# Four attention layers on one core: the last self-attention takes its output through plain values and a second projection, and two small parts of the earlier layers move

## The reference, cut to what matters

```python
x = L0(x, ctx)   # cross-attention with a causal mask, residual, LayerNorm; then gelu feed-forward
x = L1(x, ctx)   # cross-attention: scores * weights, mask; Wo, residual, LayerNorm
x = L2(x, ctx)   # cross-attention with a key mask; w_out, LayerNorm; relu feed-forward, LayerNorm
x = L3(x, ctx)   # self-attention, then a gated feed-forward
# L3, attention part (heads of 64 channels, segments of 64 tokens):
pooled = rms_norm(ctx.mean(axis=1)) ; k_c, v_c = split(pooled @ to_mem_tokens_w @ to_qkv_w)
xn = rms_norm(x, attn_norm_w)
q, k, v = split(xn @ to_qkv_w) ; q, k = rope(q), rope(k)
kf, vf = concat([k_c, persist, k]), concat([v_c, persist, v])
probs = softmax(mask(q @ kf.T * 64 ** -0.5))   # own segment, causal, plus memory and persistent keys
x = x + (probs @ vf).reshape(b, n, 1024) @ to_out_w
```

## Time and profile before

| | before |
|---|---|
| median of 3 runs | 2474.96 us (2472.53 to 2475.68) |
| the profiled execution | 2471.87 us, span 2470.1 us |
| instructions | 83369 |
| busy: TensorE matmul / weight load | 2308.8 us (93%) / 1812.7 us (73%) |
| busy: VectorE / ScalarE / GpSimd | 1888.0 (76%) / 1498.6 (61%) / 1559.2 us (63%) |
| mean granted TensorE clock | 0.985 |
| DMA moved | 211.78 MB, mean 86 GB/s |

### The profile page before, as it was taken

The page is one execution under the profiler, slowest core; times in us unless marked ns, Lnnn a source line. Parts: engine busy times, 40 slices in busy tenths (PEclk is TensorE's granted clock), DMA queues, the critical chain, the costliest instruction groups (busy, mean ns, idle before and its releaser), DMA issues.

```text
span 2470.1 us, 83369 instructions
## 1 busy us (share of the span) xinstructions
PE 2308.8 (93%) x26926; PEld 1812.7 (73%) x26926; DVE 1888.0 (76%) x4003; ACT 1498.6 (61%) x3408; POOL 1559.2 (63%) x2438
## 2 busy tenths in 40 slices
PE   7999998988888887999998989999999999999899
PEld 5777777976666665777777867777777777777687
DVE  5777772139999996777775678888888888888566
ACT  5777775549988996888885524444444444444433
POOL 2666663118999995666666766666666666666332
PEclk9999999979999998999999999999999999999999
DMA  4111111235555552222221223334333333333211
GB/s 128 43 43 42 42 42 55 72 96 164 162 162 159 165 162 49 52 50 51 50 50 52 67 76 95 93 96 97 96 94 95 94 94 95 93 94 93 54 58 53
DMA packets 443043, 211.78 MB, mean 86 GB/s; under 512 B 206400, under 2 KB 433856, under 8 KB 442816
## 3 DMA queue, kind: packets, MB, share of 16 engines
q1 hardware_dynamic: 442944, 210.51, 32.7%
HBM read 113.36 MB, written 29.88 MB: 58 GB/s over the span
## 4 chain that ended last, share of the span: by engine, by line
PE 68%; POOL 16%; issue 6%; ACT 3%; DVE 3%; DMA 2%; SPq 1%; POOLq 1%; DVEq 0%; ACTq 0%
PE bank L686 10%; PE bank L1463 9%; PE bank L1423 9%; POOL sb_region L1012 5%; PE bank L703 5%; PE bank L1491 5%; PE bank L1154 4%; PE bank L668 4%; PE bank L1168 4%; PE bank L1473 3%; PE bank L1449 3%; ACT sb_pT L774 3%; POOL sb_mean_shift L1035 2%; POOL sb_var L1024 2%; PE bank L1499 2%
## 5 line engine op out<-in xcount | busy, mean ns | idle before, releaser
L686 PE MATMUL bank<-sb_ident,sb_region 128*77 128x128 f32 x3072 | 413.1, 278 | 57.4 <-ACT sb_pT L774 54.0
L774 ACT ACTIVATE sb_pT<-bank 77x1024 f32<-77x1024 f32 x384 | 391.6, 1020 | 81.4 <-PE bank L686 80.4
L686 PEld LDWEIGHTS bank<-sb_ident,sb_region 128*77 128x77 f32 x3072 | 348.3, 151 | 112.1 <-issue 108.2
L1553 ACT ACTIVATE sb_l<-sb_l 128x640 f32<-128x640 f32 x128 | 94.5, 738 | 384.6 <-DVE sb_l L1601 384.6
L873 DVE TENSOR_REDUCE sb_max<-bank 128x8 f32<-128x616 f32 x256 | 203.1, 793 | 151.1 <-PE bank L668 80.3
L769 ACT ACTIVATE sb_region<-sb_region 128x616 f32<-128x616 f32 x384 | 276.9, 722 | 25.0 <-POOL sb_region L1012 24.9
L1680 POOL TENSOR_TENSOR sb_pn<-sb_l,sb_r_all 128x512 f32<-128x512 f32 x128 | 134.7, 1052 | 232.1 <-DVE sb_r_all L1611 224.2
L1423 PE MATMUL bank<-sb_region,sb_wqkv 128*128 128x128 f32 x2048 | 253.7, 278 | 5.8 <-DVE sb_region L1589 5.0
L1463 PE MATMUL bank<-sb_wvo,sb_region 128*64 128x512 f32 x1024 | 248.2, 606 | 0.0
L1423 PEld LDWEIGHTS bank<-sb_region,sb_wqkv 128*128 128x128 f32 x2048 | 241.9, 194 | 8.3 <-DVE sb_region L1589 5.6
L703 PEld LDWEIGHTS bank<-sb_pT,sb_v 77*32 77x32 f32 x6144 | 152.3, 110 | 93.4 <-issue 73.4
(11 more groups left out here) (184 smaller groups left out, 5629.1 us busy)
## 6 DMA issues: line engine op xcount, KB each, us to landing
sb_region<-in_side SPq DMA_DIRECT2D x64, 616.0 KB, 3.8
sb_pT<-sb_region SPq DMA_DIRECT2D x512, 64.0 KB, 2.0
sb_kF<-sb_region SPq DMA_DIRECT2D x512, 64.0 KB, 2.2
scratch_after_A<-sb_y SPq DMA_DIRECT2D x256, 64.0 KB, 1.7
sb_fx<-scratch_after_A SPq DMA_DIRECT2D x96, 128.0 KB, 2.1
sb_mask<-in_mask SPq DMA_DIRECT2D x64, 154.0 KB, 2.3
sb_x<-scratch_after_F SPq DMA_DIRECT2D x128, 64.0 KB, 1.9
sb_ctx<-in_ctxT SPq DMA_DIRECT2D x192, 38.5 KB, 1.8
```

What stands on the lines that cost most here:

```text
L686: mm = nc.tensor.transpose(two[0:C, h * T:(h + 1) * T], p_s[b.par][:, head * C:(head + 1) * C], ident[:])
L774: nc.scalar.activation(pT_s[k][:], two[0:C, :], ACT.Copy).then_inc(pT_kept.sem(b), 1)
```

## The change

1. **A3, values.** `wvo` and its folding before A1 are gone (L1778, L1860, L1829, L1864). `values` now projects plain values (all 16 heads of one 64-token segment at once, 512 columns per row of tiles, one segment per half). A new `attend_local` makes O^T, heads by tokens, in 64x64 tiles from values and transposed probabilities, right behind the scores; ScalarE copies it (`keep_outputs`), and a new `project_local` multiplies it by the output weights into the output bank, as `attend_local` did before. `wout3_turned` is a second copy of the output weights with the two halves of the rows exchanged (two more loads in A0), because two of the four tiles land on the other side. The whole output part runs half a step later: SyncE's memory values, residual and result, and VectorE's `take_out`, follow.
2. **A3, weights.** The norm's gain is applied in ScalarE's copy of xnT, so that permuted q and k weights are copies, no products; rope banks are now 3 and 6.
3. **A1, LayerNorm.** var + eps moves from GpSimd to VectorE, between `weigh` and `mask`. GpSimd no longer makes -mean * rstd but centres itself (the form of L1030 in A0 and A2), and ScalarE's centring (L820) is gone.
4. **A0, mask.** `mask_early` and L665 are gone. The scores start the banks, and eight 64x64 bf16 matmuls of 308 columns add the mask behind them, two per bank, in four different quarters of the array for each two banks. The mask is loaded in two pieces in place of one.

```diff
-            def mask_early(b, values):
-                if b.first:
+            def scores(b):
+                if ph == "A0" and b.first:
                     pe.wait_ge(masks_made, 3)
-                pe.wait_ge(k_kept.sem(b), k_kept.count(ph, b))
-                if values:
-                    pe.wait_ge(v_kept.sem(values), v_kept.count(ph, values))
-                for c in range(2):
-                    nc.tensor.matmul(bank[c][:, 0:QC], identb[:], causal[:], start=True, stop=False)
-
-            def scores(b):
                 pe.wait_ge(kblk_made.sem(b), kblk_made.count(ph, b))
                 pe.wait_ge(q_kept.sem(b), q_kept.count(ph, b))
...
-                if ph == "A0":
-                    for c in range(2, NQ):
-                        nc.tensor.matmul(bank[c][:, 0:QC], identb[:], causal[:], start=True, stop=False)
                 for c in range(NQ):
                     rows = slice(32 * c, 32 * c + 32)
                     mm = nc.tensor.matmul(bank[c][:, 0:QC], qT_s[b.par][rows, :], kblk_s[b.par][rows, :],
-                                          start=(ph != "A0"), stop=(ph != "A2"))
+                                          start=True, stop=(ph == "A1"), skip_group_check=(ph == "A0"))
+                if ph == "A0":
+                    for c in range(NQ):
+                        for g in range(2):
+                            r = (g + c) % 2
+                            rows = slice(r * KH, (r + 1) * KH)
+                            later = causal[rows, g * C:(g + 1) * C].unsqueeze(1).to_broadcast([KH, QH, C])
+                            mm = nc.tensor.matmul(bank[c][g * KH:(g + 1) * KH, 0:QC], identb[rows, r * KH:(r + 1) * KH], later,
+                                                  start=False, stop=True, skip_group_check=True)
...
-            def centre(b):
-                act.wait_ge(mean_scaled.sem(b), mean_scaled.count(ph, b))
-                wait_earlier(act, zg_made, ph, b, 2)
-                nc.scalar.activation(z_s[b.par][:], t_s[b.par][:], ACT.Identity, bias=shift_s[b.par][:, 0:1], scale=rstd_s[b.par][:, 0:1])\
-                    .then_inc(z_made.sem(b), 1)
...
+            def variance(b):
+                dve.wait_ge(mv_made.sem(b), mv_made.count(ph, b))
+                nc.vector.tensor_scalar(var_s[b.par][:], mv_s[b.par][:, 1:2], LN_EPS, None, ALU.add).then_inc(var_made.sem(b), 1)
+
             def step_weighted(b, has):
                 if has(1):
                     weigh(b + 1, 0)
                     weigh(b + 1, 1)
+                if has(-3):
+                    variance(b + -3)
...
-            def scale_mean(b):
-
-                nc.gpsimd.tensor_scalar(shift_s[b.par][:], mv_s[b.par][:, 0:1], rstd_s[b.par][:, 0:1], -1.0, ALU.mult, ALU.mult)\
-                    .then_inc(mean_scaled.sem(b), 1)
...
-                        rstd(b + -3)
-                        wait_earlier(pool, z_made, ph, b + -3, 2)
+                        root(b + -3)
                     if has(-1):
                         residual(b + -1)
                     if has(-3):
-                        scale_mean(b + -3)
+                        centre(b + -3)
...
-                    load_vom(b + 1)
-                    load_residual(b + 1)
-                if has(-1):
-                    sp.wait_ge(out3_taken.sem(b + -1), out3_taken.count(ph3, b + -1, 1))
-                    sp.dma_start(tokens(target[ph3], b + -1), y_s[(b + -1).par][:]).then_inc(y3_stored.sem(b + -1), 16)
+                if has(0):
+                    load_vom(b)
+                    load_residual(b)
+                if has(-2):
+                    sp.wait_ge(out3_taken.sem(b + -2), out3_taken.count(ph3, b + -2, 1))
+                    sp.dma_start(tokens(target[ph3], b + -2), y_s[(b + -2).par][:]).then_inc(y3_stored.sem(b + -2), 16)
...
+                    if b.first and what == "q" and eo == 1:
+                        last = Batch(GROUPS // 2 - 1, 1)
+                        pe.wait_ge(ft_made.sem(last), ft_made.count("F2", last))
                     if old.exists:
                         pe.wait_ge(roped[old_what].sem(old), roped[old_what].count(ph3, old, eo))
                     for n in range(BLOCKS):
-                        col = QPERM[what] + (eo * BLOCKS + n) * 128
-                        mm = nc.tensor.matmul(rope_bank[eo][:, n * T:(n + 1) * T], wqkv[:, col:col + 128], xnT_s[b.lap], start=True, stop=True)
...
-            def values(b, h, g):
-                if b.first and h == 0 and g == 0:
-                    last = Batch(GROUPS // 2 - 1, 1)
-                    pe.wait_ge(ft_made.sem(last), ft_made.count("F2", last))
+            def values(b, g):
+                done, done_h = (b + -2, 1) if g == 0 else (b + -1, 0)
+                if done.exists:
+                    pe.wait_ge(oT3_kept.sem(done), oT3_kept.count(ph3, done, done_h))
+                old, old_g = half_before(b, g)
+                if old.exists:
+                    pe.wait_ge(v3_kept.sem(old), v3_kept.count(ph3, old, old_g))
+                for r in range(2):
+                    mm = nc.tensor.matmul(v3_bank[r * SEG:(r + 1) * SEG, :], xnT_s[b.lap][:, g * SEG:(g + 1) * SEG], wv3[:, r], start=True, stop=True)
+                mm.then_inc(v3_made.sem(b), 1)
+
+            def outputs_ready(b, h, held):
+                pe.wait_ge(pT3_kept.sem(b), pT3_kept.count(ph3, b, h))
+
+                for v, g in held:
+                    pe.wait_ge(v3_kept.sem(v), v3_kept.count(ph3, v, g))
 
                 old, old_h = half_before(b, h)
                 if old.exists:
-                    pe.wait_ge(vo_kept.sem(old), vo_kept.count(ph3, old, 2 * old_h + g))
-                for r in range(2):
-                    mm = nc.tensor.matmul(vo_banks[g][r * SEG:(r + 1) * SEG, :], xnT_s[b.lap][:, g * SEG:(g + 1) * SEG],
-                                          wvo[:, (2 * h + r) * HC * D:(2 * h + r + 1) * HC * D], start=True, stop=True)
-                mm.then_inc(vo_made.sem(b), 1)
+                    pe.wait_ge(oT3_kept.sem(old), oT3_kept.count(ph3, old, old_h))
+
+            def attend_local(b, h):
+                for c in range(HC):
+                    for r in range(2):
+                        rows = slice(r * KH, (r + 1) * KH)
+                        for g in range(T // SEG):
+                            side = (r + g) % 2
+                            tok, col = c * T + g * SEG, (g * (H // 2) + h * HC + c) * KH
+                            mm = nc.tensor.matmul(oT3_banks[g][side * KH:(side + 1) * KH, c * SEG:(c + 1) * SEG], v3_s[b.par][rows, col:col + KH],
+                                                  pT_s3[h][rows, tok:tok + SEG], start=True, stop=True)
+                mm.then_inc(oT3_made.sem(b), 1)
...
-            def attend_local(b, h):
-                pe.wait_ge(pT3_kept.sem(b), pT3_kept.count(ph3, b, h))
-                pe.wait_ge(vo_kept.sem(b), vo_kept.count(ph3, b, 2 * h + 1))
-
-                pe.wait_ge(pp3_kept.sem(b), pp3_kept.count(ph3, b, h))
+            def project_local(b, h, leaving):
+                pe.wait_ge(oT3_kept.sem(b), oT3_kept.count(ph3, b, h))
+
+                if leaving:
+                    late, late_h = (b, 1) if h == 0 else (b + 1, 0)
+                    pe.wait_ge(pp3_kept.sem(late), pp3_kept.count(ph3, late, late_h))
+                else:
+                    old, old_h = half_before(b, h)
+                    pe.wait_ge(out3_taken.sem(old), out3_taken.count(ph3, old, old_h))
                 for c in range(HC):
                     for g in range(T // SEG):
-                        nc.tensor.matmul(out3_bank[g * SEG:(g + 1) * SEG, 0:D], pT_s3[h][:, c * T + g * SEG:c * T + (g + 1) * SEG],
-                                         vo_s[h][:, (g * HC + c) * D:(g * HC + c + 1) * D],
+                        tok = (g * HC + c) * SEG
+                        weights = (wout3, wout3_turned)[g]
+                        nc.tensor.matmul(out3_bank[g * SEG:(g + 1) * SEG, 0:D], oT3_s[h][:, tok:tok + SEG], weights[:, h * HC + c, :],
                                          start=(c == 0), stop=False, skip_group_check=True)
...
+                        attend_local(b + -1, h)
                     if leaving:
                         transpose_p(old, old_h, b + 2 if h == 0 and has(2) else None)
                     if has(2):
                         project(b + 2, "qk"[h])
-                    if has(0):
-                        values(b, h, 0)
-                        values(b, h, 1)
-                    if leaving:
-                        attend_local(old, old_h)
+                    if has(0) if h == 0 else has(1):
+                        values(b + h, 1 - h)
+                    if has(-1):
+                        project_local(b + -1, h, leaving)
 
                     following = (b, 1) if h == 0 else (b + 1, 0)
                     if has(0) if h == 0 else has(1):
                         scores_ready(*following)
-                    if leaving:
```

(42 more changed lines are left out.)

85 lines of the change are left out of this document (34 added, 51 removed).

## The result

| | before | after |
|---|---|---|
| median of 4 runs each | 2475.32 us | 2551.84 us (2544.14 to 2554.84) |
| ratio | | 1.0307 (interval 1.0283 to 1.0331) |
| span of the profiled execution | 2470.1 us | 2553.1 us |
| mean granted TensorE clock | 0.985 | 0.962 |

What follows compares the result with a forecast made beforehand. No single engine was taken to bound everything: TensorE and nearly SyncE's queue in A3, GpSimd in A1, a TensorE-ScalarE chain in A0. Terms -12 - 6 - 7 + 13 = -12 gave 2463 us; 8-in-10 range 2443 to 2486.

Steps and rivals of the forecast that it cites:

- 32 records: A3's new O^T matmuls on TensorE, directly behind the scores in the same tile shape: 0.46 us per half.
- sixteen: A3's matmul count of the old `attend_local`, whose shape, count and 0.97 us per half were carried over to `project_local`.
- A3, TensorE: A3's TensorE work per batch falls by 0.85 us, from 13.32 to 12.47 (12.9 at the worse bound).
- the row's 18 ns: Record-to-record spacing of A3's scores (0.56 / 32), used for the O^T matmuls against the skill's 25 ns minimum.
- A3, the queue: SyncE's 20 DMAs per batch keep a 12.98 us floor and become A3's bound; 0.34 per batch realised, A3 -12.
- Rival 3: A3 stays near 13.3 through a late ScalarE copy of O^T or values; total 0 to -5, 2472; chance 0.12.
- Before A1: The serial chain ahead of A1 loses the two weight folds and part of the copies: -6 us (-5 to -7).
- A0: Mask quarters cost 0.39 us per batch instead of 0.52, with +1 for added loads: -7 us in all.
- A1: GpSimd's next operations are held as before, only bare 0.19 + 0.26 and a gap go, 0.80 comes: +13 us.
- Rival 1: A1 costs nothing because the held-up time shrinks with the small operations; total -25, 2450; chance 0.17.
- Total: Whole kernel 12 us faster, 2460 on the profiled execution or 2463 on the basis of the median.
- The slower rivals: A1's GpSimd pays fully, +9 total, 2484, chance 0.12; A0's mask quarters don't overlap, +35 total, 2510, chance 0.07.

Runs made afterwards that it cites:

- e3: Kernel before the change, with eight batches instead of four in TensorE's A3 loop body, same work and order: 2524.52 us, ratio 1.0211.
- e12: Changed kernel, two-batch TensorE body in A3, VectorE's squares moved behind the first rotation, and two loads per batch issued by ScalarE: 2418.97 us, ratio 0.9778.
- e11: Changed kernel, two-batch TensorE body in A3, VectorE's squares moved behind the first rotation, all loads still on SyncE: 2448.25 us, ratio 0.9894.
- e5: Changed kernel with two batches instead of four in TensorE's A3 loop body, using one extra ScalarE copy of x^T: 2444.32 us, ratio 0.9889.
- e8: Kernel before with the change's A0 part alone, the mask as eight quarter-array matmuls behind the scores: 2469.30 us, ratio 0.9985.
- e6: Kernel before with the change's whole A1 part alone, variance on VectorE and centring on GpSimd: 2460.91 us, ratio 0.9951.
- e7: Kernel before with A1's centring moved to GpSimd and the variance left on GpSimd: 2508.80 us, ratio 1.0142.
- e4: Kernel before with longer TensorE loop bodies in the cross-attention stages: A0 ten batches, A1 twelve, A2 twelve, instead of four: 2509.96 us, ratio 1.0144.
- e9: Changed kernel with the two-batch TensorE body and two of A3's 20 DMAs per batch issued by ScalarE instead of SyncE: 2435.81 us, ratio 0.9841.

## Why the prediction was wrong, point by point

The step that failed is none of its terms but one that is missing: the size of the program. "32 records" and "sixteen" were priced in nanoseconds of TensorE and never as text that must be held. The half grows by 28 matmul records and as many weight loads, the four-batch body from 1427 to 1880 records, and past a bound between 1493 and 1787 every turn costs 8.4 to 9.0 us here. A3's loop is 82.7 us longer (720.8 - 638.1) where A3 as a whole was to be 12 shorter. Split into its two effects, that is +108 for 12 turns at 9.0 and -26 for 48 batches at 12.77 in place of 13.32; as the 9.0 was itself taken from the loop's length, this is a split and no test. The test is the chain at one turn: 3.51 and 2.17 of stall and the slow work behind them. The rest of +95.6 lies in the straight-line start (+5.1) and end (+7.8), where SyncE's issues above 0.75 us add up to 5.6 and 2.6 more than before; whether they are all of it is not shown. e3, which shares nothing with the change but the long body, shows the same stall.

- **A3, TensorE**: 12.47 forecast, 12.74 in e12. Scores and O^T were right to 0.01 (+0.47 against 0.46), and the row's 18 ns held. Mis-sized was the 0.97 for `project_local`: not its matmuls, 0.77 as before, but the passage behind them, 0.39 in h = 1 and 0.20 or 0.30 in h = 0 in place of 0.20. The queue entries of the new `outputs_ready` stand in no term of the forecast.
- **A3, the queue**: "its floor stays 12.98, so it becomes the bound": 13.04 in e11. Right, once the code fits, and only e12 against e11 proves it; e5 alone would have given the right number with the wrong certainty. Rival 3's wait (ScalarE's copies late) was there too, at the same height. With the body that fits, A3 from its first transpose of x to its end takes 870.8 (e5) against 878.4: -7.6 where I had -12.
- **Before A1**: -6 forecast (-5 to -7), -4.9 between the borders. Right.
- **A0**: -7 forecast, -3.6 in e8. Right in sign (the forecast's -7 lies just outside e8's interval of -6.4 to -1.0); the quarters cost 0.40 and lengthen the scores' part by 0.07, together 0.47 where I had 0.29 + 0.10.
- **A1**: +13 forecast, -12 in e6 and -7.7 for A1 and A2 in the changed kernel. Wrong in sign. The step: "whatever GpSimd has next will be held in the same way, so only the bare 0.19 + 0.26 go". The centring, longer than the scaled mean by 0.54, ran unheld at 801 ns, and 1.28 of held time became 0.83. In e7, with the variance left on GpSimd, the same rule came out right. Rival 1 had the mechanism, at 0.17, and it went beyond rival 1's zero.
- **Total**: without the missing term the change is worth e5's -28.6; I had -12. Between the borders of e5's own profile the gain is 4.2 in A0, 6.4 up to A1, 9.0 in A1 and A2, 2.1 in F2 and 7.6 in A3, and F3 is 1.2 longer: -28.1 together. So A1's wrong sign made the forecast gain too small, and the missing term outweighed all of it. The range of 2443 to 2486 would have held e5 and did not hold the change. The slower rivals, at 9 and 35, all sat in A1 and A0, where nothing was lost.

## What to carry to other kernels

Count an engine's instructions per loop body before and after a change, and see whether the q8 line of the profile's page grows: here a body that no longer fitted cost a fetch stall and a stretch at the lower clock at every turn, and fetches lengthened another queue's DMA issues as well, so that writing the loop out was no cure. Shorten the body first (here by one spare copy on an engine with time to spare). When two bounds stand at the same height, an experiment that removes one shows nothing; remove both before you call a bound disproved.

## What the hardware showed that I had not expected

- TensorE's loop bodies of up to 1493 records are held, those of 1787, 1874, 1880 and 2845 fetched anew at each turn, in nine 16 KB packets (thirteen for 2845). In the changed kernel's A3 that is a stall of 2.5 to 3.6 us, a second of 1.9 to 2.5, and 7 or 10 us at 1.2 GHz; at the turn of e4's A2 3.6, 0.6 and 7.
- Beside a 16 KB fetch of TensorE's text one SyncE issue takes 1.3 to 1.5 us on average in place of 0.60; without fetches none does. By what path is open, and so is why 16 of the 90 fetches of the changed kernel lengthen none.
- Small VectorE operations can be held until a GpSimd operation ends in A3 too: squares at 1.37 in place of 0.28 (21 of 44 in e9), and at 0.94 to 1.09 in all 42 of the kernel before. The Trainium skill ("SBUF — State Buffer", SBUF: two separate sides) describes an exclusive lock of a shared port pair under which the loser blocks for the whole instruction; the squares, held until GpSimd's sum of 1693.06 to 1694.33 ends, agree.
- Open: where between 1493 and 1787 the bound lies, and which order of A1's small operations meets the masks best.
